# The opening of a routed four-stage image kernel: first copies ahead of two loads, one routing later, one copy step on two queues, one set of sums behind the first MLP layer

## The reference

```
x = x + conv3x3(gn(x), sum over e of route[e] * w_experts[e]) + bias   # route = softmax(fc(mean of gn(x)))
x = x + depthwise3x3(abs(gn(x)))                                        # 0.25 around, 1 in the centre
x = x + box17x17(gn(x))                                                 # mean over 17 x 17
x = x + mlp(neighbour_sum(gn(x)))                                       # 16 -> 64 -> 64 -> 64 -> 64 -> 16 per pixel, ELU between
```

## Time and profile before

| | |
|---|---|
| median of three runs | 779.21 us |
| profiled execution | 782.74 us, span 780.0 us |
| busy: TensorE, VectorE, ScalarE, GpSimd | 82%, 79%, 73%, 26% of the span |
| mean granted TensorE clock | 0.950 |
| first matmul of layer 1 (end of the opening) | 136.83 us |
| DMA traffic | 77.10 MB, mean 99 GB/s |

### The profile page before, as it was taken

One profiled execution on the slowest core, in us unless ns is written; L12 is line 12 of the kernel. 1 busy time (PEld: TensorE's weight loads), 2 busy tenths in 40 slices (PEclk: granted clock), 3 DMA queues, 4 the chain that ended last, 5 costly groups with the idle time before them and its releaser, 6 DMA issues.

```text
span 780.0 us, 12570 instructions
## 1 busy us (share of the span) xinstructions
PE 642.8 (82%) x3886; PEld 204.7 (26%) x3886; DVE 614.4 (79%) x1102; ACT 565.8 (73%) x1081; POOL 199.7 (26%) x291
## 2 busy tenths in 40 slices
PE   0242844999989999899989998999899889899992
PEld 0121221333223332333223322332233223222220
DVE  1352775598989898889898998878887898779993
ACT  0112110689888987899889988998798878898882
POOL 1302014402540244023511352025300440140000
PEclk9975876899999999999999999999999999999996
DMA  5759488108875645263624472455340440062002
GB/s 98 137 93 178 105 179 189 38 13 155 180 142 121 149 104 118 54 146 81 152 54 108 109 161 55 110 110 134 83 93 18 111 105 1 0 149 67 1 0 54
DMA packets 69791, 77.10 MB, mean 99 GB/s; under 512 B 7650, under 2 KB 57330, under 8 KB 69746
## 3 DMA queue, kind: packets, MB, share of 16 engines
q1 hardware_dynamic: 65216, 70.72, 41.5%
q10 hardware_dynamic: 4530, 5.82, 4.1%
HBM read 9.14 MB, written 8.39 MB: 22 GB/s over the span
## 4 chain that ended last, share of the span: by engine, by line
PE 44%; DVE 22%; ACT 20%; issue 6%; DMA 5%; SPq 2%; POOL 0%; DVEq 0%; POOLq 0%
PE pz L757 13%; PE pz L751 10%; PE pc L732 9%; ACT u L609 8%; PE pc L701 8%; ACT u L617 7%; DVE g L995 7%; DMA win<-y 3%; DVE u L991 3%; DVE bn L927 3%; ACT u L614 3%; PE po L764 3%; DVE box_sum L1028 2%; DMA xs<-in_x_dram 2%; DVE g_last L995 1%
## 5 line engine op out<-in xcount | busy, mean ns | idle before, releaser
L609 ACT ACTIVATE u<-pz 128x512 f32<-128x512 f32 x472 | 275.0, 599 | 97.9 <-PE pz L751 59.4
L995 DVE SCALAR_TENSOR_TENSOR g<-u,pz 128x512 f32<-128x512 f32 x384 | 252.1, 683 | 62.5 <-ACT u L617 58.9
L757 PE MATMUL pz<-g,wT 64*64 64x512 f32 x1536 | 278.2, 610 | 15.3 <-DVE g L995 12.3
L617 ACT ACTIVATE u<-u 128x512 f32<-128x512 f32 x472 | 287.8, 638 | 1.3
L757 PEld LDWEIGHTS pz<-g,wT 64*64 64x64 f32 x1536 | 73.8, 132 | 195.9 <-issue 194.8
L751 PE MATMUL pz<-stack,wT 96*128 96x512 f32 x256 | 121.8, 615 | 2.6 <-DVE g_last L995 2.2
L732 PE MATMUL pc<-win,t 64*32 64x512 f32 x1392 | 95.4, 650 | 25.4 <-DMA win<-y 13.7
L701 PE MATMUL pc<-box_sum,box_mat 128*128 128x512 f32 x180 | 92.3, 630 | 11.0 <-DVE box_sum L1028 11.0
L927 DVE BATCH_NORM_STATS2 bn<-xs 128x6 f32<-128x512 f32 (+1 forms) x128 | 82.9, 683 | 20.2 <-DMA xs<-in_x_dram 18.3
L467 POOL TENSOR_TENSOR stat<-stat,con 128x1 f32<-128x1 f32 x32 | 22.5, 703 | 272.8 <-DVE stat L947 272.8
L995 DVE SCALAR_TENSOR_TENSOR g_last<-u,pz 128x512 f32<-128x512 f32 x128 | 82.7, 682 | 10.9 <-ACT u L617 9.3
(11 more groups left out here) (87 smaller groups left out, 366.8 us busy)
## 6 DMA issues: line engine op xcount, KB each, us to landing
win<-y SPq DMA_DIRECT2D x56, 260.0 KB, 4.2
win<-y SPq DMA_DIRECT2D x56, 195.0 KB, 4.3
out_dram<-xs SPq DMA_DIRECT2D x8, 1024.0 KB
stack<-box_sum SPq DMA_DIRECT2D x60, 128.0 KB, 3.8
stack<-near_sum SPq DMA_DIRECT2D x30, 256.0 KB, 4.0
xs<-in_x_dram SPq DMA_DIRECT2D x7, 1024.0 KB
stack<-near_sum SPq DMA_DIRECT2D x30, 192.0 KB, 3.4
win<-y ACTq DMA_DIRECT2D x8, 260.0 KB, 7.9
```

Source lines behind the costliest of these rows:

```text
L609: act.activation(u[:, m, :], pz[:, m, :], ACT.Relu, scale=-1.0, bias=0.0).then_inc(relu_done, 1)
L617: act.activation(u[:, m, :], u[:, m, :], ACT.Exp, scale=-1.0).then_inc(exp_done, 1)
L757: last = pe.matmul(pz[to, m, :], wT[rows, l, rows], g[rows, m, :], start=True, stop=True)
L995: dve.scalar_tensor_tensor(out=elus(l)[:, m, :], in0=u[:, m, :], scalar=-1.0, in1=pz[:, m, :], op0=ALU.add, op1=ALU.max).then_inc(g_writte ...
```

## The change

Five edits, all in the opening and the first round:

1. SyncE issues the first copies of sample 0 ahead of both halves of sample 1's load, and the second copies of sample 0 (line 354) ahead of sample 2's load.
2. VectorE takes `route_out(1)` ahead of sample 2's statistics, and `group_var(2, 0)`, `pool_features(2)` and `softmax_in(2)` far later: behind sample 0's third statistics and behind its box scans. TensorE, GpSimd and ScalarE follow: `group_sums(2, 0)`, `logits(2)`, `scales(2, 0)` and `softmax_exp(2)` move back.
3. Half 0 of sample 0's stack is issued by SyncE (tiles 0 and 1) and ScalarE (tiles 2 and 3); half 1 by SyncE alone.
4. `near_first` normalizes only the first half before its sums, the second half behind them.
5. `group_sums(1, 2)` on TensorE moves from the end of the opening into round 1, behind layer 1 and the convolution piece there; `group_var(1, 2)` moves behind the first ELU.

```diff
-        def stacks(eng, i, h):
+        def stacks(eng, i, h, ms=range(M)):
...
-            load_rows(1, 0, R // 2)
             sp.wait_ge(zeroed, N_ZEROED)
             windows0(sp, 0, (0,), True)
+            load_rows(1, 0, R // 2)
             load_rows(1, R // 2, R)
+            windows1(sp, 0, (0,), True)
             sp.wait_ge(x_loaded, LOAD * 3)
             load(2)
-            windows1(sp, 0, (0,), True)
...
-            stacks(sp, 0, 0)
+            stacks(sp, 0, 0, (0, 1))
+            stacks(sp, 0, 1)
...
-            stacks(act, 0, 1)
+            stacks(act, 0, 0, (2, 3))
...
+                        if first and at == 0:
+                            group_sums(1, 2)
...
-            group_sums(2, 0)
-            logits(2)
             conv_taps(0, 1, 0, range(3))
             conv_taps(0, 1, 1, range(3))
             group_sums(0, 2)
+            group_sums(2, 0, (0, 2))
             conv_taps(1, 0, 0, range(3))
             conv_taps(1, 0, 1, range(3))
+            logits(2)
...
-            group_sums(1, 2)
             rounds(pe, one)
...
                 normal3(0, 0)
-                normal3(0, 1)
                 dve.wait_ge(y3_edges, 2)
-                dve.wait_ge(y3_written, 2)
+                dve.wait_ge(y3_written, 1)
                 for c in range(2):
...
+                normal3(0, 1)
...
             softmax_in(1)
+            route_out(1)
             stats_of(2, 0, range(Q))
             merge_stats(2, 0)
-            route_out(1)
-            group_var(2, 0)
-            pool_features(2)
-            softmax_in(2)
             evacuate_pair(0, 1, 0)
...
             group_var(0, 2)
+            group_var(2, 0)
             normal2_first()
             for c in range(Q):
                 box_scan(0, c)
+            pool_features(2)
+            softmax_in(2)
```

More of the change, by code:

```diff
@@ L369, in stacks @@
             up, down = max(lo, 1), max(lo - 1, 0)
-            for m in range(M):
+            for m in ms:
                 a, b = max(2 * m - 1, 0), min(2 * m + 3, R)
@@ L374, in stacks @@
                 eng.dma_start(stack[m][4 * C:6 * C, lo:hi], y3[2 * C * m:2 * C * m + 2 * C, lo:hi, 1:W + 1]).then_inc(stack_in[h], 16)
-            eng.dma_start(stack[0][0:C, up:hi], near_sum[7 * C:P, up - 1:hi - 1]).then_inc(stack_in[h], 16)
-            eng.dma_start(stack[3][3 * C:4 * C, down:hi - 1], near_sum[0:C, down + 1:hi]).then_inc(stack_in[h], 16)
+            if 0 in ms:
+                eng.dma_start(stack[0][0:C, up:hi], near_sum[7 * C:P, up - 1:hi - 1]).then_inc(stack_in[h], 16)
+            if 3 in ms:
+                eng.dma_start(stack[3][3 * C:4 * C, down:hi - 1], near_sum[0:C, down + 1:hi]).then_inc(stack_in[h], 16)
         block = ctx.enter_context(nc.Block())
@@ L543, in _ @@
             spread(pool, 1)
+            scales(0, 2)
             scales(2, 0)
-            scales(0, 2)
             scales(1, 1)
@@ L659, in _ @@
             windows0(act, 1, (1,), False)
-            softmax_exp(2)
             for c in range(Q):
                 normal0(2, c)
+            softmax_exp(2)
             normal1(1, 0)
@@ L1063, in one @@
                         elu(t - 1, p, l)
+                        if first and at == 0:
+                            group_var(1, 2)
                         if l == 0 and part_before(t, p):
@@ L1219, in _ @@
             merge_stats(1, 2)
-            group_var(1, 2)
             rounds(dve, one)
```

## The result

Six runs of the changed kernel took 781.48 to 791.71 us, median 785.95, against 779.54 for the kernel before: ratio 1.010, 95% interval 1.0057 to 1.0143. The forecast was 776.0, with 784 as the range's upper end: **slower, and outside the range**. The profiled execution took 786.02 us, 783.2 of it span.

The account below looks back on a forecast made before the run. No engine bounds the whole span; the change touches only the opening's chain of transfer waits and VectorE work. Terms +3.1 +1.9 -1.45 -0.7 -3.7 +0.4 -2.8 = -3.25 us, giving 776.0 us, range 771 to 784.

Parts of the forecast that it names:

- What is late next: sample 2's load: Opening: VectorE stands until sample 2's load lands at 80.4 (ends 76 and 85), sums of sample 0 +3.1 us.
- Layer 1 begins at 136.0: Sign at the opening's end: 136.83 and the first five terms, -0.85; wrong if more than 4 us away.
- Arrive at the end whole: From the first layer on both programs do the same work, so the opening's gain or loss reaches the end undiminished.
- Rival 2: Opening: sample 2's load lands at 85 and the clock stays low; +5.6 us, 784.8 us; chance 0.13.
- First and second copies: Sample 0's copies: first convolution at most 0.5 us sooner; second copies landed 66.8 to 69.1, convolution 6 to 8 us sooner.
- Routing later, +1.9: Sample 2's pooling and softmax input now stand on VectorE's path to sample 1's evacuation: +1.9 us.
- The box bands' -1.45: TensorE's box bands begin later and no longer wait 2 us in their middle; second six quicker: -1.45 us.
- Neighbours' sums, sums of sample 1, clock in layer 1: VectorE additions without GpSimd beside them -0.7 us; no pause before layer 1 -3.7; layer 1 at full clock -2.8.
- The stack on two queues: Sample 0's stack, first half issued about 1.4 us earlier: worth nothing itself, must land within 15 us of issue.
- rival 4: The two queues for the stack do nothing: no effect on the sum; no chance given.
- What it feeds ... hides it: GpSimd's normalization of sample 1, now inside layers 1 and 2, costs nothing: box scans stand behind layer 2; uncovered, up to 4 us.
- The step to the median: Profiled execution 3.5 us above the runs' median; its difference of -3.25 us was carried to the median 779.2, giving 776.0.

Follow-up runs that it names:

- copies_wait: Changed kernel, with both halves of sample 1's copies issued only when sample 2's load has landed: 779.46 us, ratio 0.9997 to the kernel before.
- rows_load2: Changed kernel with sample 2's load alone issued as eight DMAs of 16 partitions, not one of 128: 776.51 us, ratio 0.9960 to the kernel before.
- halves_back: Changed kernel with the first half of sample 1's load again ahead of the first copies: 785.35 us, ratio 1.0064 to the kernel before.
- before_again: The kernel before, unchanged, run for a second profile: 782.31 us.
- routing_back: Kernel before with edits 3 to 5 alone, loads and routing of sample 2 as before: 775.73 us, ratio 0.9948.
- the two timed pairs: Edits 2 to 5 against edits 3 to 5: ratios 0.9995 and 0.9948 with the old load order, 1.0028 and 0.9983 with another.
- sums_only: Kernel before with edit 5 alone (sums and variance of sample 1 behind layer 1): 775.74 us, ratio 0.9941.

## Why the prediction was wrong

- **"What is late next: sample 2's load" failed by its size: this is the failed step.** Forecast 80.4, ends 76 and 85; measured 88.36. So the term was +10.4, not +3.1, and with it the sum of -3.25 becomes +4.05; the span grew by 3.2. The wrong choice was "SyncE's copies stay behind", taken from the issue that was held 6.99 us: the load was to run alone from 74. SyncE's first copy was held (7.41 us), but the others went out from 74.3 to 79.0, and the last of them landed at 92.4 (78.40 and 14.0), behind the load. So the load had copies beside it to its end. At the prediction's own 38 GB/s for such a load, the 0.84 MB left at 67 take 22 us, until 89: an estimate, near what was measured. The upper end of 85 let the copies end at 81, as if the load did not slow them too. In copies_wait, where the load runs alone, and in rows_load2, where it is cut, VectorE's wait falls from 22.91 to 12.40 and 14.14 us, and the loss is gone.
- **"Layer 1 begins at 136.0"** came at 142.57, beyond the 4 us that the prediction gave as its sign of being wrong. The load's term makes it 7.3 us later than forecast, the other terms 0.7 us earlier. "Arrive at the end whole" held here: from layer 2 to the end it took 634.1 us before and 634.0 now.
- **Sample 1 "complete at about 53"** came at 57: a half moved 57 GB/s, not 71. It cost nothing that the times show (halves_back).
- **Rival 2** had the mechanism and nearly the time (784.8), the time in part by luck: its landing was 3.4 us too early (+7.7, not +10.4), and it left out the clock's gain of 2.7 us, which came.
- **First and second copies**: the first convolution came 2.2 us sooner (36.88; 0.6 of it from sample 0's load), not 0.5 at most; the second at 68.55, inside 67 to 69.
- **Routing later, +1.9**: from the sums to sample 1's evacuation 10.60 us, before 9.00: +1.6. Right in this pair. The box bands' -1.45 came too (5.42), but only against one execution, and not for the reason given (before_again): from the sums of sample 0 to the last convolution it is 36.91 us in the profile before, 35.44 in the second one, 35.15 in routing_back's, 36.47 now. So the later routing costs 1.3 us by the profiles and 3.6 by the two timed pairs (some 3 us either way for each); the difference is not explained.
- **Neighbours' sums, sums of sample 1, clock in layer 1**: additions 0.69 each; no pause ahead of layer 1; 3.70 us at 1.00. Right in the changed kernel; edit 5 alone (sums_only) shows 4.6 us in the time, though there layer 1 did pause.
- **The stack on two queues, "worth nothing by itself"**, and rival 4's "no effect": before, yes, since VectorE's statistics came later. Without them in the way one queue was too slow: its copies took 17.6 us from the first issue to the last landing in sums_only (116.22 to 133.8), more than the 15 that the prediction allowed.
- **"What it feeds ... hides it" failed by 0.8 us.** GpSimd's normalization now meets the first box scan of sample 1 (VectorE, then GpSimd):

```profile
156.54 2.20 DVE L1032 TENSOR_TENSOR_SCAN box_sum<-y 128x580 f32<-128x580 f32 x1
...
162.23 1.34 DVE L1032 TENSOR_TENSOR_SCAN box_sum<-y 128x580 f32<-128x580 f32 x1
```

```profile
156.48 1.04 POOL L499 TENSOR_TENSOR y<-y,stat 128x512 f32<-128x512 f32 x1
157.48 2.10 POOL L497 TENSOR_TENSOR y<-xs,stat 128x512 f32<-128x512 f32 x1
```

  Layer 2, ahead of this scan, is 3.39 us later than before (149.25 and 145.86); the second part's first layer, behind it, 4.23 (165.46 and 161.23). At the end of the span 3.2 are left.
- **The step to the median failed.** The span grew by 3.2 us, the medians by 6.4. The profile before lay 3.2 above its median, the one after on its own: a gain read against a slow execution is partly that execution's.

## What to carry to other kernels

A transfer that is moved behind others is priced by what will run beside it until its end; give it the slow rate for all of that time, and let no in-order engine stand in front of it. Ask by how many DMA engines a load is carried before moving it: here cutting the loads gained more than any order of them. Where the argued gain is below 1%, take more than one profile of the kernel before. An edit that is worth nothing by itself can be what another one needs, as the stack's two queues for edit 5.

## What the runs showed of the hardware

- Load and copies together moved 143 GB/s; copies alone 216, the load alone 103.
- A half load had a DMA share of 0.31 and moved 57 GB/s (71 in the profile before). Whole or in pieces, a load moved some 100 with no copies beside it; in pieces it got through sooner beside copies (seen at 81.70, not 88.36).
- An issue behind a load held SyncE for 7.41 us, behind a half load for 10.07, where its neighbours take about 0.6.
- A box scan took 2.20 us beside GpSimd, 1.34 alone, and the GpSimd operation 2.10 instead of 1.04: each waited for the other once. The Trainium skill (SBUF — State Buffer, "SBUF: two separate sides") has one port pair that VectorE, with two inputs from SBUF, and GpSimd take in turn for a whole instruction; these rows agree.
- Executions of the kernel before ran from 775.94 to 785.45 us.
